# A two-layer transformer on one core: another order of chunks in attention, long GpSimd operations in quarters, routing and the experts' loads reordered

## The reference, cut to what matters

```python
h = _layernorm(x) * (1 + ca) + sa
scores = jnp.einsum('bqhd,bkhd->bhqk', q, k)
scores = scores + jnp.einsum('bqr,bkr->bqk', q_rope, k_rope)[:, None]
w = softmax(where(causal, -inf, scores / scale), axis=-1)
x = x + ga * (jnp.einsum('bhqk,bkhd->bqhd', w, v).reshape(Bb, Tt, D_MODEL) @ W_o)
...
probs = jax.nn.softmax(logits, axis=1)        # over the 2048 tokens
vals, idx = jax.lax.top_k(probs, 2)           # two of eight experts for each token
h = relu(x @ w1[e] + b1[e]); h = relu(h @ w2[e] + b2[e]); y = relu(h @ w3[e] + b3[e])
v = jnp.einsum('bse,bseo->eo' ...)            # weighted sum of y over the tokens that chose e
out = jnp.einsum('bse,eo->bso', ind, v)
...
z = jax.nn.softmax(x @ W_A.T * SCALING, axis=1)
out = jnp.einsum('bhij,bjhd->bihd', roll(z) * tril, v)
```

## Time and profile before

| | us |
|---|---|
| median of 3 executions | 1736.78 (1735.19 to 1738.25) |
| the profiled execution | 1730.19 |
| its span | 1728.5 |
| attention, first step to last | 889.7 |
| routing | 137.9 |
| experts | 211.6 |
| PE busy | 1533.4 (89%) |
| DVE busy | 1162.3 (67%) |
| ACT busy | 895.4 (52%) |
| POOL busy | 448.9 (26%) |

### The profile page before, as it was taken

One profiled execution on the slowest core, in us unless ns is written; L12 is line 12 of the kernel. 1 busy time (PEld: TensorE's weight loads), 2 busy tenths in 40 slices (PEclk: granted clock), 3 DMA queues, 4 the chain that ended last, 5 costly groups with the idle time before them and its releaser, 6 DMA issues. The chain is left out here.

```text
span 1728.5 us, 32847 instructions
## 1 busy us (share of the span) xinstructions
PE 1533.4 (89%) x12065; PEld 823.1 (48%) x12065; DVE 1162.3 (67%) x3280; ACT 895.4 (52%) x1274; POOL 448.9 (26%) x649
## 2 busy tenths in 40 slices
PE   7995989999999999999999995843999968888998
PEld 5541233333343333333333323532897835766776
DVE  3764888888788887888879813871665666111775
ACT  2440346666666666667666672431776735201453
POOL 2382536442121121211212112357200002700011
PEclk9996789999999999999999997975999978999999
DMA  8368523623315142151511113617777302784011
GB/s 310 116 193 233 145 95 105 166 78 80 128 39 119 65 80 80 39 120 65 112 48 41 63 59 124 233 65 131 131 97 101 42 8 73 260 291 176 13 37 49
DMA packets 100031, 190.43 MB, mean 110 GB/s; under 512 B 21876, under 2 KB 65908, under 8 KB 94628
## 3 DMA queue, kind: packets, MB, share of 16 engines
q1 hardware_dynamic: 80404, 113.18, 27.0%
q0 software_dynamic: 16816, 71.54, 12.2%
q10 hardware_dynamic: 2656, 3.62, 0.6%
HBM read 107.38 MB, written 80.80 MB: 109 GB/s over the span
## 5 line engine op out<-in xcount | busy, mean ns | idle before, releaser
L999 ACT ACTIVATE at_pr<-ps 128x1024 f32<-128x1024 f32 (+3 forms) x640 | 540.8, 893 | 291.5 <-PE ps L961 289.0
L1035 DVE TENSOR_REDUCE at_mx<-ps 128x1 f32<-128x512 f32 x768 | 483.7, 684 | 81.5 <-PE ps L901 79.9
L961 PE MATMUL ps<-bq,bk 64*128 64x512 f16 (+3 forms) x1280 | 291.5, 347 | 0.0
L1032 DVE CUSTOM_DVE_ANT_0 at_seen<-ps,later 128x384 bf16<-128x384 f32 (+3 forms) x512 | 229.1, 487 | 21.7 <-PE ps L901 21.4
L818 POOL TENSOR_SCALAR_AFFINE_SELECT at_pr<-at_pr 128x256 f32<-128x256 f32 x256 | 102.7, 406 | 431.6 <-ACT at_pr L999 428.5
L957 PE MATMUL ps<-sqk 64*128 64x512 f16 (+3 forms) x1280 | 210.9, 352 | 1.2 <-ACT at_pr L999 0.7
L957 PE MATMUL ps<-at_sqk 64*128 64x512 f16 (+3 forms) x1280 | 203.5, 347 | 1.5 <-ACT at_pr L999 1.3
L901 PE MATMUL ps<-sqk 64*128 64x512 f16 (+3 forms) x640 | 177.7, 378 | 25.7 <-DVE at_mx L1035 13.4
L901 PE MATMUL ps<-at_sqk 64*128 64x512 f16 (+3 forms) x640 | 163.2, 351 | 4.2 <-DVE at_mx L1035 3.7
L939 PE MATMUL ps<-at_pr,at_vl 128*32 128x512 f32 (+3 forms) x1280 | 150.0, 540 | 1.8 <-POOL at_pr L818 1.6
L939 PE MATMUL ps<-at_pr,vl 128*32 128x512 f32 (+3 forms) x1280 | 150.2, 541 | 0.1
(11 more groups left out here) (301 smaller groups left out, 2271.4 us busy)
## 6 DMA issues: line engine op xcount, KB each, us to landing
d_rows<-at_nil POOLq DMA_DIRECT2D x31, 1064.5 KB
mi_tz<-d_z SPq DMA_DIRECT2D x32, 1024.0 KB, 7.0
ex_xr<-d_rows SPq DMA_DIRECT2D x39, 256.0 KB, 11.4
d_va<-st_va SPq DMA_DIRECT2D x8, 1024.0 KB, 4.3
d_o<-at_oc POOLq DMA_DIRECT2D x32, 256.0 KB, 2.4
at_pw<-in_w POOLq DMA_DIRECT2D x24, 256.0 KB, 3.5
d_w<-at_ph POOLq DMA_DIRECT2D x24, 256.0 KB, 2.4
exw<-d_w SPq DMA_DIRECT2D x8, 768.0 KB, 12.7
```

The lines of the kernel that those rows point to most:

```text
L961: ins = pe.matmul(ps[:, 2 * f + r, off:CH], g.bk[half[r], b, k], g.bq[half[r], b, q], start=False, stop=True)
L999: act.activation(pr[:, n % 2, f, :, off:CH], ps[:, 2 * f:2 * f + 2, off:CH], ACT.Exp, scale=INV_SCALE).then_inc(exp_done[f], 1)
L1032: ins = dve.tensor_tensor_reduce(seen[:, turn, r, 0:n], src, g.later[:, CH - n:CH], 1.0, LOWEST, ALU.add, ALU.max, dst)
L1035: ins = dve.tensor_reduce(dst, src, AX.X, ALU.max)
```

## The change

1. Start: the two fills of lines 275 and 276 are issued as eight pieces of 128 x 512 each.
2. Attention: the units 2 to 7 take their chunks in the order 2, 3, 1, 0 instead of 3, 2, 1, 0; unit 0 has that order already, unit 1 keeps 3, 2, 1, 0. The planner's constant FETCH is 6500 instead of 5400. Everything that `schedule()` places follows from these two: ahead of their first step, chunks 2 and 3 of unit 0 have 62 and 21 maxima, the first chunk of unit 1 has 4, the second chunk of unit 2 (chunk 3) has 13, and no other chunk has any. The turn of the next unit's first chunk stands in the second or third step of chunk 1 in units 2 to 6 (the fifth in unit 1), that of its second chunk in the eighth step of its first (the eleventh in unit 2). SP's queue keeps its order: first shift, 13 loads, three shifts.
3. Routing: POOL's multiply (line 1203) is issued in four pieces of 128 x 256. On DVE, softmax(0) goes ahead of normalise(6), picks(0) ahead of normalise(7), and positions(0) behind normalise(7), ahead of low(5); on PE, probabilities(0) goes to the end of n = 4 (ahead of the eighth projection) and counts(0) to n = 5, behind its gate.
4. Experts: SP's request for a chunk's rows is split from the packing of its weights. Chunk 0's rows are asked for ahead of the biases; then rows are asked for up to three chunks ahead of the packing, but no further than chunk 8 until chunk 9's packing is due.
5. Mix: each of POOL's two operations (lines 1801 and 1804) is issued in four pieces of 16 x 512.

```diff
--- before.py
+++ after.py
@@ -272,8 +272,11 @@
             ins.then_inc(gate_used, 1)
             rope(3)
             pool.wait_ge(gate_used, 2)
-            pool.memset(g.sqk[0][:, 0, :, 1, :], 0.0).then_inc(blank, 1)
-            pool.memset(g.sqk[0][:, 1, :, 1, :], SHIFT_UNIT).then_inc(blank, 1)
+            for s, value in enumerate((0.0, SHIFT_UNIT)):
+                for i in range(2):
+                    for it in range(NCH):
+                        ins = pool.memset(g.sqk[0][:, s, i, 1, it * CH:(it + 1) * CH], value)
+                ins.then_inc(blank, 1)
             rope(4)
             for x in range(2):
                 pool.wait_ge(stored[x], 16 * NST * (NCH // 2))
@@ -568,8 +571,8 @@
 
 
     NU = NG * NB
-    OPENING, FALLING = [2, 3, 1, 0], [3, 2, 1, 0]
-    ORDER = [OPENING] + [FALLING] * (NU - 1)
+    INWARD, FALLING = [2, 3, 1, 0], [3, 2, 1, 0]
+    ORDER = [INWARD, FALLING] + [INWARD] * (NU - 2)
     STEPS = [attn_steps(o) for o in ORDER]
     PAIRS = [max_pairs(o) for o in ORDER]
     ENDS = [{qc: n for n, (qc, kb) in enumerate(st)} for st in STEPS]
@@ -606,7 +609,7 @@
     def chunk_maxima(v, m):
         return [("max", v, k, r) for k in range(upto(v, m), upto(v, m + 1)) for r in range(2)]
 
-    HEAD_STEP, AHEAD, FETCH, SLACK = 6, 2, 5400, 100
+    HEAD_STEP, AHEAD, FETCH, SLACK = 6, 2, 6500, 100
 
     def ticks(w):
         return w * 0.4167
@@ -1200,7 +1203,12 @@
             pool.memset(zeros[:, :], 0.0).then_inc(set_up, 1)
             for n in range(N):
                 pool.wait_ge(o_ld[n % NO], 16 * 2 * KT * (n // NO + 1))
-                pool.tensor_tensor(ou[:, n % NO], ou[:, n % NO], rb[:, n % NO], ALU.mult).then_inc(on_ready, 1)
+                for k in range(KT):
+                    for j in range(2):
+                        part = slice(j * C, (j + 1) * C)
+                        ins = pool.tensor_tensor(ou[:, n % NO, k, part], ou[:, n % NO, k, part], rb[:, n % NO, k, part],
+                                                 ALU.mult)
+                ins.then_inc(on_ready, 1)
             pool.wait_ge(w_ready, 2 * N)
             pool.memset(ind3[:, :, :], 0.0).then_inc(set_up, 1)
             pool.wait_ge(lo_ready, NCH)
@@ -1361,13 +1369,14 @@
                 if n + 2 < N:
                     add(n + 2)
                     statistics(n + 2)
+                    if n == NCH:
+                        softmax(0)
+                    if n == NCH + 1:
+                        picks(0)
                     normalise(n + 2)
-                if n == NCH:
-                    softmax(0)
                 if n == NCH + 1:
-                    picks(0)
+                    positions(0)
                 if n == NCH + 2:
-                    positions(0)
                     sure_chunks()
                     thrice(0)
                 low(n)
@@ -1486,8 +1495,6 @@
                     ins = pe.matmul(ps[0:E, 6, :], gw[:, k, :], hf[:, n % 2, k, :], start=(k == 0), stop=(k == KT - 1))
                 ins.then_inc(gate_done, 1)
                 if n == NCH + 1:
-                    probabilities(0)
-                if n == NCH + 2:
                     counts(0)
                 if n:
                     pe.wait_ge(lo_ready, n)
@@ -1496,6 +1503,8 @@
                         o = (t % 2) * C + k * P
                         ins = pe.transpose(ps[:, 4 + t // 2, o:o + P], hf[:, n % 2, k, t * P:(t + 1) * P], g.ident[:, :])
                 ins.then_inc(back_done, 1)
+                if n == NCH:
+                    probabilities(0)
             probabilities(1)
             counts(1)
             pe.wait_ge(ind3_ready, NB)
@@ -1528,6 +1537,7 @@
         XB = 6
         NW = 8
         LAG = 3
+        EARLY = 3
         bias = sb("bias", [P, 3, KT, NCK])
         ball = sb("ball", [E, P, 3, KT])
         wb = sb("wb", [P, NW, CX])
@@ -1582,20 +1592,32 @@
                 sp.dma_start(wb[:, a:a + n, :], g.d_ws[a:a + n, :].rearrange("a n -> (a n)").unsqueeze(0).bitcast(F32)
                              .to_broadcast([P, n * CX])).then_inc(wb_ld[p % (NW // 2)], 16)
 
-            sp.dma_start(ball[:, :, :, :], g.i["b"]).then_inc(b_ld, 16)
-            for cc in range(NCK):
+            rows = {}
+
+            def fetch(cc):
                 x = cc % XB
                 at = sp.value_load(g.start[0:1, cc:cc + 1], min_val=0, max_val=E * RG)
-                rows = g.d_rows[bass.ds(at, CX), :]
+                rows[cc] = g.d_rows[bass.ds(at, CX), :]
                 if cc >= XB:
                     sp.wait_ge(turned, cc - XB + 1)
                 if cc == SURE:
                     sp.wait_ge(again, 16 * NT)
-                sp.dma_start(xr[:, x], rows[:, 0:C].rearrange("(t p) c -> p t c", p=P)).then_inc(x_ld[x], 16)
+                sp.dma_start(xr[:, x], rows[cc][:, 0:C].rearrange("(t p) c -> p t c", p=P)).then_inc(x_ld[x], 16)
+
+            def pack(cc):
                 if cc >= NW:
                     sp.wait_ge(wb_ld[cc // 2 % (NW // 2)], 16 * (cc // NW))
-                sp.dma_start(g.d_ws[cc % NW].unsqueeze(1), rows[:, C:C + 1], allow_slow_non_contiguous=True)\
+                sp.dma_start(g.d_ws[cc % NW].unsqueeze(1), rows.pop(cc)[:, C:C + 1], allow_slow_non_contiguous=True)\
                   .then_inc(packed[cc % NW], 16)
+
+            fetch(0)
+            sp.dma_start(ball[:, :, :, :], g.i["b"]).then_inc(b_ld, 16)
+            fetched = 1
+            for cc in range(NCK):
+                while fetched <= min(cc + EARLY, NCK - 1 if cc >= SURE else SURE - 1):
+                    fetch(fetched)
+                    fetched += 1
+                pack(cc)
                 if cc % 2 and cc >= LAG:
                     spread((cc - LAG) // 2)
             for p in range((NCK - LAG) // 2, -(-NCK // 2)):
@@ -1798,10 +1820,16 @@
                 pool.wait_ge(rec_ready, b + 1)
                 if b:
                     pool.wait_ge(z_st[b - 1], 32)
-                pool.tensor_scalar(zn[:, :], z[:, b, :], zrec[:, b:b + 1], None, ALU.mult).then_inc(zn_ready, 1)
+                for it in range(NCH):
+                    cols = slice(it * CH, (it + 1) * CH)
+                    ins = pool.tensor_scalar(zn[:, cols], z[:, b, cols], zrec[:, b:b + 1], None, ALU.mult)
+                ins.then_inc(zn_ready, 1)
                 pool.wait_ge(zn_ready, b + 1)
                 pool.wait_ge(zh_ready, b + 1)
-                pool.tensor_tensor(zhl[:, 1, :], zn[:, :], zhl[:, 0, :], ALU.subtract).then_inc(zl_ready, 1)
+                for it in range(NCH):
+                    cols = slice(it * CH, (it + 1) * CH)
+                    ins = pool.tensor_tensor(zhl[:, 1, cols], zn[:, cols], zhl[:, 0, cols], ALU.subtract)
+                ins.then_inc(zl_ready, 1)
             pool.wait_ge(bias_ready, 1)
             pool.wait_ge(hn_ready, N)
             for t in range(NB * NT):
```

## The result

The changed kernel takes 1713.62 us, median of 4 executions, beside 1735.99 of the kernel before, median of 4: a ratio of 0.9884 (0.9845 to 0.9923). The prediction was 1722.7, in a range of 1710 to 1732: 14 us less were forecast, 16 to 22 us less were measured.

What follows compares the result with a forecast made beforehand. PE was taken to set attention's pace, with blocks of maxima at unit starts, and a chain of waits routing's. Attention -9.6, routing -2.8, experts -0.5 and mix -1.2 gave -14.1 us: 1736.8 to 1722.7, range 1710 to 1732.

Steps and rivals of the forecast that it cites:

- Boundaries, -17.4: Attention, starts of units 2 to 7: the new order removes the blocks of maxima at six boundaries, 17.4 us less.
- The stop in unit 2, +4.5: Attention, unit 2: 13 maxima poured ahead of chunk 3 cost 4.5 us, bounds 2.7 to 7.8.
- FETCH, +3.3: Attention: the longer planner constant pours seven more maxima in units 0 and 1, costing 3.3 us, at most 4.3.
- Loads ahead of chunk 3's shift, 0: Attention, SP's queue: the unit's loads go ahead of chunk 3's shift but leave 4 us of cover, costing nothing.
- quarters, +0.4: Routing: POOL's multiply in four pieces takes 0.4 us more each; only one, at the phase's start, counts.
- mix, -1.2: Mix: with POOL's operation in pieces DVE's normalising gains 2.8 us or nothing; 1.2 less taken, bounds 0 and -3.7.
- Routing's order, -3.2: Routing: moving softmax and picks earlier starts positions(0) sooner, by 3.3 us, or 2.4 at half clock; 3.2 taken.
- Experts, -0.5: Experts: early row requests gain little because chunk 9 waits for the second scatter; 0.5 us less, bounds -3 and +3.
- Pieces let DVE in: Rival, mix and routing: DVE gets in after one piece, 4 to 5 us more gained, 1718; chance 0.14.
- Attention gives it back: Rival, attention: steps with more maxima stall on banks, returning 7 us in six units, 1730; chance 0.16.
- Chunk 3's shift late: Rival, attention units 2 to 6: shift rows land late behind the loads, 1748 at 5 us each; chance 0.07.
- It doesn't do what it says: Rival, attention: boundary blocks stay because ScalarE or the output's move is late; only routing gains, 1733; chance 0.04.

Runs made afterwards that it cites:

- e5: Kernel before with only the new chunk order in units 2 to 7, FETCH left at 5400: 1724.86 us beside 1733.42, ratio 0.9948.
- e7: Kernel before with the attention part alone (FETCH 6500), unit 1 also in order 2, 3, 1, 0: 1726.22 us beside 1733.42, ratio 0.9968.
- e2: Kernel before with only the pieces (memsets, routing's multiply, mix's two operations): 1733.92 us beside 1734.82, ratio 0.9997.
- e3: Kernel before with only routing's order changed on DVE and PE: 1727.86 us beside 1734.82, ratio 0.9968.
- e6: Kernel before with the change's routing order, but PE's transposes of the probabilities behind the eighth projection: 1729.49 us beside 1733.42, ratio 0.9965.
- e4: Kernel before with only the experts' rows asked for ahead: 1725.58 us beside 1734.82, ratio 0.9964.
- e11: Kernel before with rows asked for ahead, but each chunk's weights packed ahead of the further requests: 1733.70 us beside 1732.43, ratio 1.0008.
- e10: The changed kernel itself measured again, on another chip, against the kernel before: 1716.46 us beside 1732.43, ratio 0.9898.

## Why the prediction was right or wrong, point by point

- **The bound.** Right: taking PE's blocked stretches at the boundaries away shortened attention, and the units 4 to 6 came out at 102.91 (forecast 102.6 to 103); unit 3, behind the long unit 2, took 104.1.
- **Boundaries, -17.4.** With FETCH 5400 (e5) attention is 10.5 us shorter from first to last exponential (846.4 to 835.9), and unit 2 is 5.7 us longer there than unit 3 (109.8 against 104.1), so the boundaries gave 16.2. Against a unit 2 that follows an inward unit (102.91, e7) the stop is 6.9 and the boundaries gave 17.4; the split depends on which unit one compares with, the sum doesn't.
- **The stop in unit 2, +4.5.** It was 5.7 with FETCH 5400 and 6.8 with 6500 (110.9 - 104.1), within its bounds (2.7 to 7.8), or 6.9 and 8.0 against 102.91, the last just outside; the clock in it was 0.77. **FETCH, +3.3:** it was 2.1, of which unit 2's part is 1.1. Together: -16.2 + 5.7 + 2.1 = -8.4, where -9.6 was forecast.
- **Loads ahead of chunk 3's shift, 0.** Right. In unit 4 the shift's DMAs were issued at 652.10, 19.5 us into the unit, and no wait at the score product for them appears in the waits. That the same loads would hold up POOL's copies in unit 1, had that been turned inward, was not seen (e7); it bears on the rival of that name, which was looked for on SP's queue alone.
- **Start, 0; quarters, +0.4; mix, -1.2.** Start and mix: e2 shows no gain in time. Mix's -1.2 was the mean of two cases, and neither came: DVE waits out neither one piece nor the whole row, but one piece at each operation, which makes the four 0.8 us shorter. The last three operations at 80.04 had shown that way of alternating. The +0.4 is too small for any run here to show.
- **Routing's order, -3.2.** The mechanism was right, down to the projection at half clock (6.60 us, forecast "near" 6.6). The size is 4.1 (1.4 and 2.5 in the two kernels with the slowest projection, of which the first profile of the changed kernel is the 2.5). What the sum left out is that DVE's normalising(6) now comes before POOL's fill of line 1205: 1.38 us in e3 and in the changed kernel, 3.24 in e6, where it met the fill.
- **Experts, -0.5: the step that failed.** It said that "whatever PE gains until there it waits there", because chunk 9 needs the second scatter. But PE's wait for chunk 9 was 1.14 us, and a wait that short is no proof that rows cannot come earlier. They were there by 50.8 when PE was. The gain is 6 us or more (e4, and the table), outside the term's own bounds of -3 and +3. By the waits the limit that takes over is the spread of the weights; the one try at it (e11) lost the gain instead.
- **The rivals.** Pieces let DVE in: its sign came (in mix, and in routing's quarters too, a DVE operation waits out one piece; it takes 1.2 to 1.3 us there and 0.8 here), its 4 to 5 us did not (e2). The Trainium skill's rule (SBUF — State Buffer, "Who interferes with whom") says that the instruction that issues first holds the pair to its end. The trace agrees in mix, where pieces and DVE's operations alternate, and disagrees in the start, where a waiting DVE operation stayed out for 5.12 us while some ten memsets of POOL began and ended. Attention gives it back: no, PE's waits of the maxima fell from 17.0 to 13.8 us. Chunk 3's shift late: no. It doesn't do what it says: no.
- **The signs that were named.** Units 4 to 6 and unit 2 were as said, unit 0 was 1.8 us longer. Unit 1 was not 1 to 3 us longer but 4.4 shorter, since the boundary to unit 2 lies in it. The first scatter came 1.4 us earlier in the first profile and 2.0 in e10, below or at the edge of the 2 to 4 named; e3 alone had 4.4. And the turn of chunk 9 came 94.3 us after the first scatter, where it was 99.7: the sign of the experts' term was wrong as the term was.
- **The sum.** -14.1 forecast, -15.8 in the profiled spans and -16 to -22 in medians. The experts gave 5.5 us more and routing 1.3 more (4.1 as in e3 and e10; the first profile has less), mix and attention 1.2 and 1.2 less: -18.5, and the rest is within the spread of the runs. That the spans come within 1.7 us of the forecast is luck: from barrier to barrier the experts' stage gave 6.1 us where the prediction had ruled out more than 3, and made up for attention (8.5 for 9.6), routing (1.4 for 2.8), mix (0 for 1.2) and a start that was 2.3 us longer.

## What to carry to other kernels

When engines compute ahead into a few buffers, look for the place where the work ahead is poured in a row: in this kernel the order of the chunks was worth 10.5 us of attention there (e5), since a shorter first piece buys the lead. Before calling a later wait the cap of an earlier gain, ask how long that wait is and whether what it waits for could have come sooner. And look at what stands in front on a DMA queue, not only at how early a request is made: here the rows had to go ahead of the word-sized packing (e11).

## What the hardware showed that was not expected

- A row of short GpSimd operations can hold DVE in two ways: the first normalising stayed out for 5.12 us through a row of memsets of 0.5 us (3.4 in e2), while in mix each operation waited out one piece of 1.2 us in turn, 4.30 us for four.
- Rows asked for behind a transfer of 256 words came 6 us later (turned at 12.8 against 6.5 us) though asked for only 0.7 us later.
- The same wait of PE, 3.16 us, was followed by 5.2 us of projection in some executions and by 6.6 in others (full clock: 3.62). A wait of 2.84 us was followed by 3.72 us of projection, one of 1.97 by 5.41.
